# A mixture-of-experts and recurrence kernel: the recurrence in groups of two tokens, its tables in PSUM, and the copy of x two gathers sooner

## The reference

```python
x = x + 0.5 * ffn(layernorm(x), gate_w, w1, w2)
x = x + recurrence(layernorm(x), a_params, B_w, C_w, D)
x = x + 0.5 * ffn(layernorm(x), gate_w, w1, w2)
...
# ffn: top-1 of E = 8 experts per token, at most CAP = 160 tokens each (in order of token), F = 512
expert_idx = argmax(softmax(tokens @ gate_w)); pos = cumsum(one_hot(expert_idx)) - 1
h = relu(expert_input @ w1[e]); out[token] = prob[token] * (h @ w2[e])
# recurrence, per batch: 128 states, W a rotation in the Fourier domain (|lambda| = 1)
h[t] = ifft(lambdas * fft(h[t-1])) + B_w @ u[t];   y[t] = C_w @ h[t] + D * u[t]
```

## Time and profile before

| | |
|---|---|
| median of 3 runs | 151.71 us (151.61 to 152.92) |
| profiled execution | 150.5 us, span 148.6 us, mean granted clock of TensorE 0.967 |
| busy share of the span | PE 86%, PEld 65%, DVE 59%, ACT 38%, POOL 38% |
| chain that ended last, by engine | PE 46%, DMA 14%, issue 10%, ACT 9%, POOL 7%, DVE 5%, SP's queue 4% |

### The profile page before, as it was taken

How to read it: one execution, slowest core, us unless ns; L and a number is a source line. 1 busy time by engine, 2 the same in 40 slices (tenths; PEclk the granted TensorE clock), 3 DMA queues, 4 the chain that set the end, 5 groups by cost and what they waited for, 6 DMA issues and landing times.

```text
span 148.6 us, 2493 instructions
## 1 busy us (share of the span) xinstructions
PE 128.5 (86%) x749; PEld 96.6 (65%) x749; DVE 88.2 (59%) x379; ACT 56.1 (38%) x156; POOL 56.0 (38%) x96
## 2 busy tenths in 40 slices
PE   5988989699799989379999999999989969999920
PEld 2315334289699965137887788778976249999810
DVE  1198787994467431257679668988894133755310
ACT  2522434235353302055756675752010035553200
POOL 3490002777205778001212211231100677665570
PEclk9999999999999999999999999999995599999995
DMA  4999995236660111690013441344024312211110
GB/s 89 305 351 401 350 290 144 55 108 185 194 203 22 57 53 53 213 321 35 2 45 101 146 133 39 123 148 146 0 76 158 91 46 56 56 38 40 43 45 18
DMA packets 15740, 18.49 MB, mean 124 GB/s; under 512 B 1904, under 2 KB 10608, under 8 KB 15600
## 3 DMA queue, kind: packets, MB, share of 16 engines
q1 hardware_dynamic: 13936, 15.34, 32.7%
q0 software_dynamic: 1280, 2.66, 6.3%
q10 hardware_dynamic: 512, 0.34, 0.9%
HBM read 12.70 MB, written 7.73 MB: 138 GB/s over the span
## 4 chain that ended last, share of the span: by engine, by line
PE 46%; DMA 14%; issue 10%; ACT 9%; POOL 7%; DVE 5%; SPq 4%; POOLq 1%
PE pair L1062 9%; PE pair L1075 9%; ACT u L520 7%; DMA w1s<-w 5%; PE pair L1158 5%; POOL xg L370 5%; PE pair L1149 4%; SPq L292 3%; PE pair L1180 3%; PE pair L1182 3%; PE pair L943 2%; DMA xg<-x,tok 2%; DMA x<-x_scratch 2%; DMA xg<-x_scratch,tok 2%; PE pair L1087 2%
## 5 line engine op out<-in xcount | busy, mean ns | idle before, releaser
L943 PE MATMUL pair<-warm_in,ones_bf 128*128 128x512 bf16 x61 | 18.9, 457 | 3.9 <-DMA x<-x_scratch 2.3
L1062 PE MATMUL pair<-xcT,w1s 128*128 128x160 f32 x128 | 20.5, 303 | 0.6 <-ACT xcT L452 0.6
L1062 PEld LDWEIGHTS pair<-xcT,w1s 128*128 128x128 f32 x128 | 18.0, 190 | 1.7 <-ACT xcT L452 1.7
L460 ACT ACTIVATE hT<-pair 128x320 f32<-128x320 f32 x32 | 13.8, 435 | 13.6 <-PE pair L1062 12.1
L1075 PE MATMUL pair<-hT,w2s 128*128 128x160 f32 x112 | 17.8, 302 | 0.0
L370 POOL DMA_INDIRECT xg<-x,tok x10 | 10.2, 1019 | 16.7 <-issue 16.7
L1075 PEld LDWEIGHTS pair<-hT,w2s 128*128 128x128 f32 x112 | 15.6, 190 | 0.0
L370 POOL DMA_INDIRECT xg<-x_scratch,tok x10 | 10.1, 1007 | 13.7 <-DMA x_scratch<-x 10.9
L943 PEld LDWEIGHTS pair<-warm_in,ones_bf 128*128 128x128 bf16 x61 | 6.8, 117 | 12.2 <-issue 4.1
L402 POOL TENSOR_TENSOR vb<-vq,st 128x128 f32<-128x128 f32 x8 | 3.8, 474 | 27.0 <-ACT vq L495 27.0
L381 POOL DMA_INDIRECT x_scratch<-xnew,tok x10 | 9.9, 985 | 10.3 <-DMA x_scratch<-x 7.6
(11 more groups left out here) (190 smaller groups left out, 242.8 us busy)
## 6 DMA issues: line engine op xcount, KB each, us to landing
x_scratch<-x SPq DMA_DIRECT2D x8, 272.0 KB, 2.1
xt<-x_turned SPq DMA_DIRECT2D x8, 256.0 KB, 6.1
w1s<-w SPq DMA_DIRECT2D x2, 1024.0 KB, 9.0
w2s<-w SPq DMA_DIRECT2D x8, 256.0 KB, 6.7
x_scratch<-x SPq DMA_DIRECT2D x8, 256.0 KB, 3.4
x<-x_scratch SPq DMA_DIRECT2D x8, 256.0 KB, 4.8
out<-x SPq DMA_DIRECT2D x8, 256.0 KB, 2.6
ce<-const_early ACTq DMA_DIRECT2D x1, 330.0 KB, 4.6
```

Source lines behind the costliest of these rows:

```text
L460: nc.scalar.activation(hT[:, e % 2, half * HC:(half + 1) * HC, :], bank[4 + half][:, 0:HC * CAP] .rearrange("p (c s) -> p c s", c=HC), ACT ...
L943: M(bank[to][:, :], ones_bf[:, :], warm_in[:, :], start=True, stop=True)
L1062: ins = M(bank[4 + half][:, c * CAP:(c + 1) * CAP], w1s[:, i, ch * P:(ch + 1) * P], xcT[:, i * CAP:(i + 1) * CAP], start=True, stop=True)
```

## The change

**Groups of two (TR = 2).** A batch has NG = 256 groups. Tokens 4p to 4p + 3 are two groups (half h = 0, 1 of a partition), and column (p, h) of the new tables is group 2p + h. All of vq, vb, va, z, zc, zs, ct, st are 256 wide. group_sums is two matmuls of 256 columns that read uT as "d p h": neighbouring columns are 1 KB apart. within is two halves, each 288 + 144 columns, and read_out one matmul of 272 columns a half; the state is written permuted, so that each half's columns lie together (state_out). within(b) and read_out(b) now stand behind group_sums(b+1). uT has three buffers.

**Tables in PSUM.** va is written over the sums in bank 5; the sines table for zs is copied once to bank 7 (st_near), and zs is written there. So group_sums(b) waits for z of batch b - 1, where it waited for va.

**Statistics.** They are kept in x1's own rows (XP = D + 6 = 134 wide now, so that x1 is loaded in pieces of 512 bytes), and made three batches ahead instead of two; stats(2) and shift(2) stand before the loop. ScalarE makes the u's of a batch in two halves around turned_part.

**x2 of two batches by TensorE.** add_rows(6) and add_rows(7) with a copy by ScalarE each replace add_back(6); rank(1, 1) stands between them.

**Copy of x.** Piece b of the fill waits for gather b + 1 instead of b + 3. The powers p0 to p4 move from ahead of the FFN's tiles into the slots between them, and nine warm-up matmuls stand behind the first load of x1 instead of 14.

Two names in the order below: `pair` is a PSUM bank, `ce` the identity. On VectorE, in front of the loop and at va(0), where before there stood

The core of the diff:

```diff
-    NG = SEQ // TB
+    TR = 2
+    NG = SEQ // TR
...
-        x1 = sb("x1", [P, NT, D])
+        x1 = sb("x1", [P, NT, XP])
...
-        zs = sb("zs", [P, NG])
+        st_near, zs = bank[7][:, 0:NG], bank[7][:, NG:2 * NG]
...
+        def by_group(a):
+            return a[:, 0:NG].rearrange("s (p h) -> s p h", h=2)
+        def state_out(b):
+            return state[:, b % 2, :].rearrange("s (h p) -> s p h", h=2)
...
-        dve_steps = [steps("i0 i1 i2 i3 i4 d0 ...
+        dve_steps = [steps("p0 p1 i0 p2 i1 p3 i2 p4 i3 i4 d0 ...
...
-                sp.wait_ge(d_gather[min(b + 3, NS - 1)], 16)
+                sp.wait_ge(d_gather[b + 1], 16)
                 sp.dma_start(tiles(x1_dram, b), tiles(x_rows, b)).then_inc(d_fill, 16)
...
+            normalise(1, 0, TB // 2)
+            deviation(2)
             for i in range(NB):
                 if i + 1 < NB:
                     copy_uT(i + 1)
-                if i + 2 < NB:
-                    deviation(i + 2)
+                if i + 3 < NB:
+                    deviation(i + 3)
+                if i + 2 < NB:
+                    normalise(i + 2, 0, TB // 2)
                 if i + 1 < NB:
                     turned_part(i + 1)
                 if i + 2 < NB:
-                    normalise(i + 2)
+                    normalise(i + 2, TB // 2, TB)
...
-                V.tensor_tensor(va[:, :], bank[5][:, 0:NG], ct[:, 0:NG], ALU.mult).then_inc(va_r, 1)
+                V.tensor_tensor(bank[5][:, 0:NG], bank[5][:, 0:NG], ct[:, 0:NG], ALU.mult).then_inc(va_r, 1)
...
-                    ins = V.tensor_tensor(zs[dst, :], z[src, 0:NG], st[src, 0:NG], ALU.mult)
+                    ins = V.tensor_tensor(zs[dst, :], z[src, 0:NG], st_near[src, :], ALU.mult)
...
-                V.tensor_tensor(state[:, b % 2, :], zc[:, :], zs[:, :], ALU.add).then_inc(state_r, 1)
+                V.tensor_tensor(state_out(b), by_group(zc), by_group(zs), ALU.add).then_inc(state_r, 1)
...
+            stats(2)
+            shift(2)
             for i in range(NB):
                 turn_back(i)
-                if i + 2 < NB:
-                    stats(i + 2)
+                if i + 3 < NB:
+                    stats(i + 3)
...
                 pe.wait_ge(uT_sb, b + 1)
                 if b >= 1:
-                    pe.wait_ge(va_r, b)
-                for c in range(TB):
-                    ins = M(bank[5][:, 0:NG], vt[:, TB - 1 - c, :],
-                            uT[:, b % 2, c * P:(c + 1) * P], start=(c == 0), stop=(c == TB - 1))
+                    pe.wait_ge(z_r, b)
+                by_residue = uT[:, b % 3, :].rearrange("d (h r p) -> d r p h", h=2, r=TR)
+                for r in range(TR):
+                    ins = M(bank[5][:, 0:NG].rearrange("s (p h) -> s p h", h=2), vt[:, TR - 1 - r, :],
+                            by_residue[:, r, :, :], start=(r == 0), stop=(r == TR - 1))
                 ins.then_inc(v_ps, 1)
...
+            add_rows(LAST - 1)
+            rank(1, 1)
             add_rows(LAST)
-            rank(1, 1)
```

More of the change, by code:

```diff
@@ L265, in macaron_moe_ssm_kernel, with rated_with @@
         GROUPS = [[(0, NS)], [(0, NS // 2), (NS // 2, NS)]]
+        RATED = [(b * TB, (b + 1) * TB) for b in range(NB)]
+        def rated_with(b):
+            return b
         def group(n, i):
@@ L807, in _ @@
             carried_table()
-            powers(ct, st, 0, 5)
             slots(0)
+            dve.wait_ge(turns, 1)
+            V.tensor_copy(st_near, st[:, 0:NG])
             outward_tables()
@@ L915, in _ @@
                     gate_back(i - 1)
[L916 to L917 removed]
+                if i + 3 < NB:
+                    shift(i + 3)
                 if i == NB // 2:
@@ L1187, in read_out @@
-            def read_out(b):
-                pe.wait_ge(state_r, b + 1)
-                y = y_pair(b)
-                for h in range(2):
-                    ins = M(y[:, h, E:E + 2 * PITCH], state[:, b % 2, :],
-                            gt[:, 2 * h:2 * h + 2, :].rearrange("p r c -> p (r c)"), start=False, stop=True,
-                            skip_group_check=True)
-                ins.then_inc(y_ps, 1)
+                M(y[:, h, 0:TR * BLOCK], uT[:, b % 3, 2 * h * P:(2 * h + 1) * P], tab[:, :, :].rearrange("p r c -> p (r c)"),
+                  start=True, stop=False, skip_group_check=True)
@@ new lines, in within, with read_out @@
+                ins = M(y[:, h, BLOCK:2 * BLOCK], uT[:, b % 3, (2 * h + 1) * P:(2 * h + 2) * P], tab[:, 0, :],
+                        start=False, stop=False, skip_group_check=True)
+                if h == 1:
+                    ins.then_inc(lag_ps, 1)
+            def read_out(b, h):
+                pe.wait_ge(state_r, b + 1)
+                ins = M(y_of(b)[:, h, :, :], state[:, b % 2, h * P:(h + 1) * P], gt[:, :, :], start=False, stop=True,
+                        skip_group_check=True)
+                if h == 1:
+                    ins.then_inc(y_ps, 1)
```

256 lines of the change are left out of this document (117 added, 139 removed).

## The result

The changed kernel takes 155.62 us against 151.66 before (medians of four runs each): 1.0226 times the time, with a 95% interval of 1.0151 to 1.0300. It is slower, by more than the 1% that I had called telling; my forecast was 152.7, no change, in a range of 149.8 to 155.8. The range held, the forecast didn't. Some runs of most kernels show a lower clock or a longer time than the rest (one of the four here took 163.92): the ratios leave these slow runs out, while a time in us is the median of all runs, so that the two don't always fit each other. The profiled execution of the changed kernel took 155.89, its span is 154.1, 5.5 above before's 148.6.

A forecast was written before the change was run, and what follows sets the result against it. VectorE was to become the bound at 4.64 us a batch, over the ring's 4.54. Terms 1.9 - 1.1 + 0.5 + 0.5 - 0.8 = +1.0 on 150.5 gave 151.5, in the median's terms 152.7 (no change); range 149.8 to 155.8.

The forecast's parts named there:

- The start: Start of the loop: va(0) waits for batch 2's shift, batch 1's sums wait for z; va(1) 1.9 us later.
- Batches 1 to 4: Loop's first part: three turns of 4.65 us in place of 5.02, together -1.1 us.
- The end: Last state and what follows it: wider scan, zs and state, partly covered, +0.5 us.
- my dear 1.3: Sign for the group sums on TensorE: 0.9 us together as forecast, 1.3 or more if the read is dear.
- the copy of x: Ahead of the loop: copy two gathers sooner, first scatter 0.75 to 1.2 us sooner; net of x1's load -0.8.
- My fourth rival: Earlier copy shares the queues with gathers and weights, scatters start no sooner: +0.8 us, 153.5; chance 0.05.
- The landing of x1: Load of x1 in pieces of 512 bytes because its rows got longer: 0 to 0.5 us more.
- Rival 3: TensorE's clock falls at the loop's start, between the sums of batches 0 and 1: about +2.5 us, 155.2; chance 0.08.
- batches 4 to 7: Loop's later part: wider work on VectorE, less idle time and earlier last statistics, 0.3 to 0.7, taken as +0.5 us.
- the ring: TensorE and ScalarE in a batch, from transposes through sums, vq and u's to the next transposes: 5.02 to 4.54 us.
- The strided read: Group sums on TensorE read columns 1 KB apart: +0.06 us a batch, between nothing and +0.43.
- rival 1: Strided read dear in group sums: +0.43 a batch gives 154.3, twice the time 157.1; decides from 0.16; chance 0.22.

The follow-up runs named there:

- a_busy: The changed kernel with matmuls whose results nobody uses in all thin stretches of TensorE: 155.06 us, 1.0247 of before.
- a_stats: The changed kernel with statistics, deviation and shift of batch 2 behind va(0), those of batches 3 and 4 behind va(1): 160.08 us, 1.0588 of before.
- a_read: The changed kernel with the state written contiguous and the group sums reading uT contiguous, which mixes up the groups: 157.77 us, 1.0346 of before.
- b_copy1: The kernel before with only piece b of the copy of x waiting for gather b + 1: 152.78 us, 1.0003 of before.
- a_again: The changed kernel timed once more, unaltered: 157.35 us, 1.0313 of before.
- a_warm: The changed kernel with more unused warm-up matmuls while x1 is awaited and at the loop's start: 157.62 us, 1.0434 of before.
- a_flat: The changed kernel with the state written contiguous and its halves picked at the read-out's weight load: 158.22 us, 1.0412 of before.
- a_three: The changed kernel with the copy behind gather b + 3, x1 in dense rows and TensorE's thin stretches filled: 153.06 us, 1.0110 of before.

## Why the prediction came out as it did

**Right.** The start: I had 1.9 us for the wait on the shift and for the sums behind z; with the clock held (a_busy) it is 2.13, and a_stats shows that va(0) comes 1.9 us sooner without batch 2's statistics and shift ahead of it. Batches 1 to 4: -1.1 foretold, -0.98 measured. The end: +0.5, measured +0.53. The state near 0.5: it is 0.61, the upper end (0.292 + 0.135 + 0.17). Of the signs that I named, the late va(0) and the turn without idle time came; the first scatter before 44.8 and the clock of 1.00 did not, and the sums, 1.24 in the loop's middle, lie nearer to my dear 1.3 than to 0.9; but even contiguous (a_read) they last 1.03, so my marks for them were too low.

**Luck: the range.** 155.62 lies just inside 155.8, but that end stood for a read at 0.43 a batch or a fallen clock worth 2.5 us. The read cost 0.21 and the clock 1.2; the rest of the way up came, in the profile, from the copy and the landing, for which I had no price so high.

**Wrong in most profiles: the copy of x.** I let the first scatter move forward to the first result, and left the first result where it was. A transfer of the copy that moves forward moves beside the gathers, and the result can move back: last gathered tile 41.71 and 41.45 with b + 1, 40.12 and 40.81 with b + 3. That the two compete is read from these times; no run shows where. My fourth rival had the copy share the queues, and only made the gain nothing. Against -0.75 to -1.2 stands +0.92 in the profile, +0.66 in b_copy1, and -0.73 in a_again, where the gathers weren't delayed; in the runs it is not to be told from nothing. The landing of x1 in 512-byte pieces was just over my upper end of 0.5, 0.55 to 0.58. Together they cost 1.50 where I had -0.8: this step was 2.3 us off in the profiled execution, the largest part of what I missed.

**Wrongly weighed: the clock.** Rival 3 had the mechanism and one of the two places, a fall where TensorE has 5 us with one set of transposes, with 2.5 us and a chance of 0.08. In the loop's first part the clock fell in all seven profiles of the changed order that didn't fill these stretches, and in none of the four of the kernel before and its variants; it cost 1.2 us in the first trace (a_busy). The other place lies ahead of the loop, behind the wait for x1, which the landing made longer (2.92 instead of 2.33); with that wait filled (a_warm) the first fall came at 67.5 instead of 64.5. The five warm-up matmuls less, which I put at nothing, may have a part in it; no run takes them alone. I should have given this rival most of the chance. What makes the clock fall stays open in part: in a_stats it held behind a wait of 2.98 us for x1, and at 108 to 110 us TensorE was busy 0.64 of 2 us in the changed kernel and the clock held to 118.

**Mis-sized: batches 4 to 7.** +0.5 foretold, +1.05 measured. About 0.5 us of it, nearly all that I had too little, is two operations of the counting, which took 0.54 and 0.61 where they had taken 0.29 and 0.38. In the changed kernel both began while GpSimd's vb ran:

```profile
96.35 0.73 POOL L420 TENSOR_TENSOR vb<-vq,st 128x256 f32<-128x256 f32 x1 [1.60 <-ACT vq L512]
...
96.69 0.54 DVE L648 TENSOR_TENSOR is_top<-x,top 128x128 bf16<-128x128 f32 x1
...
101.02 0.73 POOL L420 TENSOR_TENSOR vb<-vq,st 128x256 f32<-128x256 f32 x1 [1.80 <-ACT vq L512]
...
101.29 0.61 DVE L658 TENSOR_TENSOR chosen<-key,top_key 128x128 bf16<-128x128 bf16 x1
```

In the kernel before and in a_read, where vb ran beside neither, they took 0.29 and 0.38 to 0.39. My sum had no term for this. The widths were nearly right: in the loop's middle VectorE's turn is 4.69 instead of 4.64, with the state 0.10 over my half and the rest a little under.

**Right for a wrong reason: the bound of the loop.** I had VectorE at 4.64 and the ring at 4.54, and named VectorE. a_flat took 0.18 off VectorE and nothing off the turn. The strided read was the term that I had too low: +0.06 foretold, 0.21 measured (a_read), so the ring is 4.67; that is past the 0.16 from which rival 1 had the read decide. By the pace of the strided weight load I took it for nearly hidden; by the ratio of single loads it would have been 0.43. The measured price lies in the middle. The Trainium skill's rule ("SBUF — State Buffer", Specifications), two hits in a line of 16 bytes for full bandwidth, agrees with it in sign: the new read alternates between two rows of columns 1 KB apart, so no two neighbours share a line, and 1024 columns cost 1.28 instead of 1.06, far from twice.

**In sum** 1.0 was forecast against 5.5 in the profiled execution: the copy and the landing account for 2.3 of the difference, the clock for 1.2, batches 4 to 7 for 0.55, the start for 0.2, the loop for 0.1; in the medians it is 4.0 against 1.0, and no run says how these shares lie there. a_three, with the copy, the landing and the clock taken away, stands 1.7 us (1.1%, between 0.6% and 1.6%) above before: what is left, the loop in groups of two with its late start and longer end, is slower by itself.

## What to carry to other kernels

Price a transfer that moves forward on both sides: what it releases, and what it now runs beside. An order that left TensorE thin for some us lost its clock here in seven of seven profiles, just where the next work waited for it; fill such a stretch, or count the fall as the likely case. And before a loop is rebuilt, take the one idea that shortens its ring and try it alone: here two u's out of the ring, with the deviation and the shift moved to allow it, gave -0.42 us in each of three turns without any of the rest.
